# The second head's masked decays before the state updates, and the step-size projection with high and low weights side by side

## What is computed

```python
zxbcdt = einsum('bld,ed->ble', u, W_in)
dt = softplus(zxbcdt[..., -NHEADS:] + dt_bias)      # 8 columns: one step size for each head
# xBC: causal convolution over 4 tokens, then silu; x: 8 heads x 128, Bm and Cm: 64 each
dA = dt * A                                          # A < 0, one for each head
Lmat = exp(cum[s] - cum[z]) for z <= s, else 0       # cum: running sum of dA in a chunk
Y_diag = einsum('bcshn,bczhn,bchsz,bczhp->bcshp', Ch, Bh, Lmat, xdt)
states = einsum('bczhn,bchz,bczhp->bchpn', Bh, decay_states, xdt)
s_next = s * chunk_decay + states                    # carried from chunk to chunk
Y_off  = einsum('bcshn,bchpn,bchs->bcshp', Ch, prev_states, exp(cum))
y  = Y_diag + Y_off + x * D
yn = rmsnorm(y * silu(z)) * norm_w;  out = yn @ W_out.T
x  = layernorm(x + out)
```

## Time and profile before

| | |
|---|---|
| median of 3 runs | 1405.49 us (1405.03 to 1407.62) |
| the profiled execution | 1405.99 us, of it 1404.2 us from the first to the last instruction |
| PE busy | 1362.4 us, 97% of the span |
| DVE busy | 1070.9 us, 76% |
| ACT busy | 802.1 us, 57% |
| POOL busy | 649.9 us, 46% |
| one block of the first layer, 419 to 511 us | 92 us: PE busy 90.10, DVE 74.51, ACT 58.13, POOL 52.66 |
| the second layer, 760 to 1404 us | 644 us: PE busy 634.88, DVE 468.05 |
| first 60 us | PE busy 51.30, DVE 48.66 |

### The profile page before, as it was taken

One profiled execution on the slowest core, in us unless ns is written; L12 is line 12 of the kernel. 1 busy time (PEld: TensorE's weight loads), 2 busy tenths in 40 slices (PEclk: granted clock), 3 DMA queues, 4 the chain that ended last, 5 costly groups with the idle time before them and its releaser, 6 DMA issues.

```text
span 1404.2 us, 27260 instructions
## 1 busy us (share of the span) xinstructions
PE 1362.4 (97%) x9574; PEld 888.9 (63%) x9574; DVE 1070.9 (76%) x1848; ACT 802.1 (57%) x1593; POOL 649.9 (46%) x628
## 2 busy tenths in 40 slices
PE   8899999999999999999999999999999999999998
PEld 4455555555555555556556777777777777777774
DVE  7887877886877879878775887767776767777775
ACT  6686574773856828748565555555455545545441
POOL 0574264673663736625355544434343434434331
PEclk9899999999999999999999999999999999999999
DMA  8436334263342532424325130111101010110002
GB/s 258 160 125 212 127 106 105 80 171 87 105 128 84 164 108 84 143 91 136 124 87 196 61 106 16 47 45 46 34 28 61 31 63 16 59 33 31 31 24 68
DMA packets 101342, 129.16 MB, mean 92 GB/s; under 512 B 40401, under 2 KB 61265, under 8 KB 100049
## 3 DMA queue, kind: packets, MB, share of 16 engines
q1 hardware_dynamic: 101200, 127.35, 29.3%
HBM read 99.93 MB, written 27.39 MB: 91 GB/s over the span
## 4 chain that ended last, share of the span: by engine, by line
PE 60%; issue 13%; DVE 12%; ACT 8%; POOL 6%; DMA 1%; ACTq 0%; POOLq 0%; SPq 0%; DVEq 0%
PE ring L1110 15%; PE p_turn L1090 8%; PE p_y L1090 7%; PE ring L873 7%; PE p_seg L1090 6%; PE p_st L1090 5%; PE ring L902 5%; DVE acc L1806 2%; ACT p_seg L1333 2%; ACT xdt L1324 2%; PE p_y L946 2%; PE p_y L954 2%; DVE seg L1904 1%; POOL sq_sum L1634 1%; DVE st L1918 1%
## 5 line engine op out<-in xcount | busy, mean ns | idle before, releaser
L873 PE MATMUL ring<-u_split,weights 128*128 128x512 f16 x1620 | 376.2, 382 | 2.1 <-DVE x_ch L1811 1.9
L873 PEld LDWEIGHTS ring<-u_split,weights 128*128 128x128 f16 x1620 | 155.6, 99 | 172.2 <-issue 8.0
L1717 POOL TENSOR_TENSOR xdt<-xdt 128x512 f32<-128x512 f32 x64 | 100.2, 1566 | 351.8 <-DVE xdt L2160 351.8
L1806 DVE SCALAR_TENSOR_TENSOR acc<-ring,taps,acc 128x511 f32<-128x511 f32 (+2 forms) x192 | 143.7, 749 | 4.5
L902 PE MATMUL ring<-w_out,raw 128*128 128x512 f16 x672 | 147.1, 379 | 0.0
L1324 ACT ACTIVATE xdt<-p_turn,dts 128x128 f32<-128x128 f32 x256 | 73.0, 376 | 84.9 <-PE p_turn L926 84.9
L1626 POOL TENSOR_TENSOR raw<-yg,raw 128x512 f16<-128x512 f32 x64 | 78.7, 1230 | 79.2 <-ACT raw L1354 78.6
L902 PEld LDWEIGHTS ring<-w_out,raw 128*128 128x128 f16 x672 | 65.7, 98 | 77.8
L1621 POOL TENSOR_TENSOR yg<-y_ch,z_ch 128x512 f32<-128x512 f32 x64 | 81.9, 1280 | 44.1 <-DVE y_ch L1926 44.1
L1333 ACT ACTIVATE p_seg<-cum_rows,cum 128x128 f32<-128x128 f32 x256 | 80.8, 388 | 6.2 <-DVE seg L1904 6.2
L1277 ACT ACTIVATE ring<-acc 128x512 f32<-128x512 f32 x64 | 38.5, 602 | 80.0 <-DVE acc L1806 79.6
(11 more groups left out here) (420 smaller groups left out, 3367.7 us busy)
## 6 DMA issues: line engine op xcount, KB each, us to landing
cum_rows<-cum_dram SPq DMA_DIRECT2D x64, 256.0 KB, 4.1
quant<-in_w_ffn SPq DMA_DIRECT2D x24, 512.0 KB, 4.4
quant<-in_w_ffn SPq DMA_DIRECT2D x48, 256.0 KB, 4.1
cum_g<-cum_dram SPq DMA_DIRECT2D x64, 128.0 KB, 4.4
rows<-in_u_tok SPq DMA_DIRECT2D x32, 256.0 KB, 3.7
x_dram<-rows SPq DMA_DIRECT2D x32, 256.0 KB, 2.0
tern_ug<-quant SPq DMA_DIRECT2D x32, 256.0 KB, 3.5
u_raw<-in_u_t SPq DMA_DIRECT2D x7, 1024.0 KB, 8.4
```

What stands on the lines that cost most here:

```text
L873: mm = pe.matmul(bank_k[:, :], w_in[:, ws, k, col:col + P], us[:, par, k * T:(k + 1) * T], start=(i == 0), stop=(i == 3 * KD - 1))
L1717: pool.tensor_tensor(tile_[:, 1, :, :], tile_[:, 0, :, :], tile_[:, 1, :, :], ALU.mult).then_inc(hid_ok, 1)
L1806: dve.scalar_tensor_tensor(acc[:, buf, k + 1:T], own[:, 0:T - 1 - k], taps[:, h, 2 - k:3 - k], acc[:, buf, k + 1:T], ALU.mult, ALU.add).th ...
```

## The change

Three things. First, in every slot (the prologue's too) DVE does the second head's `seg` before the three state updates instead of after them. Second, both step-size projections multiply the high tokens with the high and the low weights in one matmul of 16 columns, and only the low tokens with the high weights alone: 16 matmuls of 128x16 and 16 of 128x8 instead of 48 of 128x8. The sums of high and of low weights then lie in separate columns of `p_turn`. Third, `dt_first` reads both: a second DVE operation of 128x32 adds the low sums to `dt_x`, behind a new semaphore `dt_high`; `p_turn` is freed only after it.

```diff
             def dt_proj(n, par, use):
 
                 pe.wait_ge(u_lo_ok, n + 1)
                 wait(pe, turn_free, use)
                 for c in range(C):
-                    i = 0
-                    for us, ws in ((u_hi, 0), (u_lo, 0), (u_hi, 1)):
+                    for us, parts in ((u_hi, 2), (u_lo, 1)):
                         for k in range(KD):
-                            mm = pe.matmul(p_turn[:, c * H:(c + 1) * H], us[:, par, k * T + c * P:k * T + (c + 1) * P],
-                                           w_in[:, ws, k, COL_DT:COL_DT + H], start=(i == 0), stop=(i == 3 * KD - 1))
-                            i += 1
+                            mm = pe.matmul(dt_out(c, parts), us[:, par, k * T + c * P:k * T + (c + 1) * P],
+                                           w_in[:, 0:parts, k, COL_DT:COL_DT + H], start=(us is u_hi and k == 0),
+                                           stop=(us is u_lo and k == KD - 1), skip_group_check=True)
...
                 for c in range(C):
-                    for us, ws in ((u_hi, 0), (u_lo, 0), (u_hi, 1)):
+                    for us, parts in ((u_hi, 2), (u_lo, 1)):
                         for k in ks:
...
             def dt_first(n, use):
                 dve.wait_ge(turn_full, use + 1)
-                dve.scalar_tensor_tensor(dt_x[:, :, :], p_turn[:, 0:C * H].rearrange("p (c h) -> p c h", c=C), INV,
+                both = p_turn[:, 0:2 * C * H].rearrange("p (c s h) -> p c s h", c=C, s=2)
+                dve.scalar_tensor_tensor(dt_x[:, :, :], both[:, :, 0, :], INV,
                                          dt_bias[:, :].unsqueeze(1).broadcast_to([P, C, H]), ALU.mult,
+                                         ALU.add).then_inc(dt_high, 1)
+                dve.wait_ge(dt_high, n + 1)
+                dve.scalar_tensor_tensor(dt_x[:, :, :], both[:, :, 1, :], INV, dt_x[:, :, :], ALU.mult,
                                          ALU.add).then_inc(turn_free, 1)
...
             conv(0, 0, 3)
+            within(0, 0, 1, 1)
             for c in range(C - 1):
                 state_update(0, 0, 1, c)
-            within(0, 0, 1, 1)
             silu(0, 3)
...
                     if state_slot(n, p):
+
+                        within(n, par, p, 1)
                         for c in range(C - 1):
                             state_update(n, par, p, c)
-                        within(n, par, p, 1)
```

More of the change, by code:

```diff
@@ L319, in build @@
         turn_free = sem("turn_free")
+        dt_high = sem("dt_high")
         dt_v = sem("dt_v")
@@ L826, in _, with dt_out @@
         def _(pe):
+            def dt_out(c, parts):
+                return p_turn[:, 2 * c * H:(2 * c + parts) * H].rearrange("p (s h) -> p s h", s=parts)
             def dt_proj(n, par, use):
@@ L991, in _ @@
                 for c in range(C):
-                    for us, ws in ((u_hi, 0), (u_lo, 0), (u_hi, 1)):
+                    for us, parts in ((u_hi, 2), (u_lo, 1)):
                         for k in ks:
[L994 to L997, removed]
+                            mm = pe.matmul(dt_out(c, parts), us[:, 0, k * T + c * P:k * T + (c + 1) * P],
+                                           w_in[:, 0:parts, k, COL_DT:COL_DT + H],
+                                           start=(half == 0 and c == 0 and k == 0 and us is u_hi),
+                                           stop=(k == KD - 1 and us is u_lo), skip_group_check=True)
                 if half:
```

## The result

The changed kernel takes 1401.39 us at the median (1395.44 to 1403.84, 20 runs), the kernel before 1405.50 (20 runs). The ratio is 0.9966, 95% interval 0.9958 to 0.9974: faster by 4.1 us between the medians, 3.7 to 5.9 by the interval, where 11 were forecast and the range ended at 1400. The profiled execution took 1401.63 us, with 1399.9 us from the first to the last instruction.

What follows compares the result with a forecast made beforehand. The prediction took PE, held by loads waiting for DVE's `seg`, as the bound. Its terms, -6.3 - 2.8 - 2.1 + 0.25 = -10.95 us, took 1405.99 to 1395.0, less 0.5 for the median: 1394.5 us, range 1388.5 to 1400.

Steps and rivals of the forecast that it cites:

- What bounds the kernel: PE, busy 97% of the span; its L946 loads wait 28 times for DVE's `seg`, 20.1 us in total.
- Part 1: `seg` ahead of the states on DVE comes 1.02 us earlier, shrinking each wait by at most that; at most 19.0 us.
- the gates: One block followed through its slots: part of PE's lead is given back, leaving about 1.05 us each for blocks 2 to 7.
- the wait at L962: Sign: PE waits about 1 us for POOL's `sq_sum` in each block, giving back 0.9 to 1.1 us of its lead.
- Block 7: Counted among the six steady blocks, 2 to 7: about 1.05 us gained from the order, between 0.9 and 1.21.
- Block 1: Two waits of 1.02 us count and the clock stays up: 2.8 us gained, 2.1 if the clock falls all the same.
- Start and block 0: Prologue and block 0 are held by DVE: PE gains nothing there, and the second `dt_first` operation costs 0.25 us.
- Part 2: Step-size projection, 32 matmuls for 48: saves 0.35 us in each of six blocks, 2.1 us, between 0 and 2.4.
- The rival of the weight loads: In the projection each removed matmul saves its 96 ns load, 1.5 us a block: 1387.4 us in all; chance 1%.
- Part 3: Second DVE operation of `dt_first`: 0.22 us, covered in the six steady blocks; +0.25 us taken for prologue and start.
- The sum of squares takes it all: At L962 POOL's chain doesn't move, so only the projection's 2.1 us and block 1's 2.8 at most remain: 1401; 8%.

Runs made afterwards that it cites:

- the repeat: The changed kernel itself run and traced once more, nothing altered: 1400.72 us against 1406.46 for the kernel before, ratio 0.9959.
- the filled kernel: The changed kernel with six superfluous 128x512 matmuls ahead of PE's wait for the sum of squares in blocks 1 to 6: 1398.45 us, ratio 0.9948.
- the used: The changed kernel with the step-size projection ahead of the sum of squares on PE in blocks 1 to 6: 1394.32 us, ratio 0.9909.
- the removed wait: The changed kernel with the split of the next block's tokens one place later on ACT and DVE in slot 1: 1389.41 us, ratio 0.9891.
- the lengthened wait: The kernel before with one unused POOL operation ahead of each block's last addition to `sq_sum`: 1414.67 us against 1406.46, ratio 1.0057.

## Why the prediction was wrong

- **What bounds the kernel, and Part 1 up to the gates: right.** The load's wait was the cost: 28 waits of 20.1 us became 3.4 us, `seg` comes straight after `x_ch`, L958 waits for no state, and DVE never waits for ACT's exponential at a second head.
- **The gates: right, the gain of a block slightly low.** The lead is given back at the sum of squares, in each block, and its wait was announced as a sign (about 1 us; the loads waited 1.0 to 1.75). The 0.3 that was to remain in slot 3 did not: in blocks 2 to 6 PE waits for `seg` only once, on the loop's way back. Without a drop, stretch 2 takes 90.2 instead of 91.77 (the repeat and the filled kernel): 1.55, of which 0.40 is the projection. That leaves 1.15 for the order, against 1.05 taken, inside 0.9 to 1.21.
- **The step that failed: what the wait at L962 does to the clock.** I used the clock once, to count the drop that would go in block 1. I didn't ask the same question of the wait that I had just predicted myself; the sum put the clock's part behind L962 at nothing, without a reason. The loads' wait there grew from 0.65 to 1.6 us, PE's idle time from at most 0.3 to between 1.1 and 1.3 (in five of the six), and behind it PE works on the output projection and what stands in it for some 26 us without a pause (408.75 to 434.54 us in the first trace), where a drop counts in full. Three drops at 1.69 are 5.1 us in the profiled run; 3.7 on average over the runs by the mean clocks. Of the 6.6 us between -10.95 and -4.3 this is the main part. The traces with the filled, the used and the removed wait (no drop in blocks 1 to 6) and with the lengthened wait of the kernel before (three) show it. How many drops a run gets is chance: the fastest of the 20 runs came within 1 us of the forecast.
- **Second term: the loop's way back, in block 3.** No term of the sum had it. Stretch 3 without a drop (the repeat) took 93.47 us, 0.6 more than before instead of 1.4 less. On the way back, in the middle of stretch 3, DVE stands with nothing to wait for:

```profile
378.01 1.41 DVE L1934 SCALAR_TENSOR_TENSOR y_ch<-x_ch,d_skip,p_y 128x512 f32<-128x512 f32 x2 [4.09 <-issue]
```

  From there DVE works without a pause up to the next second head's `seg` (385.13), and PE, which waited for `seg` nowhere else in blocks 2 to 6, waits for this one:

```profile
385.87 1.16 PE L950 MATMUL p_y<-seg,xdt 128*128 128x128 f32 x8 [1.46 <-DVE seg L1912]
```

  In the kernel before the pause was 2.58, and PE itself stood 1.61 at the same point, so that part of it was covered. In the other traces DVE's pause was 2.8 to 4.5 us, nearly the same in two traces of one kernel (4.09 and 4.02; 2.93 and 2.79), and with the new order stretch 3 is longer than stretch 2 by 1.9 to 3.7 us, the more the longer the pause. It goes with the program and not with the run. That the pause is what costs the 2 us is argued from these rows, which show 1.5 of them; no experiment took it away, and why its length changes stays open.
- **Block 7: mis-sized.** 1.05 forecast; the stretch to the end gained 0.3 in the first trace and lost 0.2 in the repeat. The stretch has the second layer in it, which blurs this. From the seventh sum of squares to the last block's (L1131 before, L1135 now) it is 81.76 us before and 81.29 after, and 81.75 to 81.78 in all traces with the old order and 81.29 to 81.31 in all with the new: 0.46 is what the order gives there. Why not more was not followed.
- **Block 1: mis-sized.** Both waits went or shrank and the clock stayed up, but the stretch gained 2.3 and not 3.15. The projection alone, with the old order and no drop, took 94.10 there, 1.15 less than before; of this 0.40 is the projection, so the drop cost about 0.75, near the 0.7 forecast. From 94.10 to the changed kernel's 92.96 the order gives 1.14, and not 2.1: the second wait's gain is given back at the sum of squares, as in the other blocks. Nor is it shown that the order removed the drop: it stands in two of the four traces with the old order (before, and the longer wait) and in none of the eight with the new.
- **Start and block 0: wrong in sign, small.** +0.25 forecast, -0.6 measured, with a drop at 31 to 36 us less. That drop came back with the order alone, with the projection ahead of the sum of squares and in one trace of the later split, and three traces with the old order don't have it, so it isn't the change's.
- **Part 2: the saving 0.40 a block instead of 0.35.** 16 columns cost as much as 8. The floor that the Trainium skill gives for 1 to 64 columns ("TensorE: Matmul & The Clock Gate", section "Back-to-back issue gap") holds, with 25 ns in both rows. The rival of the weight loads is out: 16 fewer of them saved 0.40, not 1.5.
- **Part 3: right.** 0.22 us, covered by a pause that is still 1.51.
- **The rivals.** None of them happened. "The sum of squares takes it all" gave nearly the right time, 1401, by a wrong mechanism: POOL's chain did move (the drop-free stretches gain 1.15 from the order). The time came out there by luck, because the clock and the loop's way back took what the chain had left.

## What to carry to other kernels

When an engine's small waits are removed, ask where its lead will be collected: at the next place where it waits for a chain that didn't get faster, all at once. If that engine is PE and a long stretch of matmuls follows, one wait of 1.6 us (1.1 of PE's time) can cost 1.7 more through the clock, where the four short ones of a block did not; put needed work into it, or shorten the chain that it waits for (here by moving one operation past another on ACT and DVE, 12 us off the changed kernel). And look at the mean clock of the runs, not only at their median: here it fell by 0.0026, and that is 3.7 us.

## What the runs showed of the hardware

- Of six waits of PE's loads at the sum of squares (1.0 to 1.75 us), three were followed by a drop of the granted clock to half in the first trace and two in the second, one of them behind the same wait. Two traces of one kernel with the same wait to 0.01 us (1.13 and 1.12 idle) differed in that.
- Each drop lasted about 3.5 us at 1.2 GHz, and cost 1.69 us where PE had a backlog.
- A 128x16 fp16 matmul passes in the same 25 ns as a 128x8 one.
- Over all twelve traces a drop followed 11 of 21 waits at that place in which PE stood 0.87 to 1.26 us, and none of 51 in which it stood 0.83 us or less.
- POOL's 128x512 `raw` takes 1.16 us, and 2.05 beside DVE's 128x2048 split; apart from it, 1.17.
- DVE's pause on the loop's way back was 2.6 to 4.5 us, by program.
